# Decoder layer on one core: low key parts of the score products padded with zero rows to 128, one buffer for attended rows, scorer row reloaded per batch

## What is computed

```python
h = x * rsqrt(mean(x * x, -1) + EPS) * norm_w        # x is layer-normed before
q, k, v = proj(w_q), proj(w_k), proj(w_v)            # 16 heads of 64
ll = where(causal, einsum('qd,kd->qk', q, k) * 64 ** -0.5, NEG)
scores = h @ scorer_w + scorer_b
idx = top_k(scores, 128)                             # these keys count a second time
attn = softmax(concat([ll, ll at idx]))
o = attn[:512] @ v + attn[512:] @ v[idx]
x = x + x + o @ w_out                                # layer-normed x inside
```

## Time and profile before

| | us |
|---|---|
| three runs: median (lowest, highest) | 2413.64 (2413.43, 2414.61) |
| profiled execution: span from first to last instruction | 2414.0 |
| PE busy in the span | 2241.6 (93%) |
| DVE busy | 1349.6 (56%) |
| ACT busy | 845.5 (35%) |
| POOL busy | 429.2 (18%) |

### The profile page before, as it was taken

How to read it: one execution, slowest core, us unless ns; L and a number is a source line. 1 busy time by engine, 2 the same in 40 slices (tenths; PEclk the granted TensorE clock), 3 DMA queues, 4 the chain that set the end, 5 groups by cost and what they waited for, 6 DMA issues and landing times. The chain is left out here.

```text
span 2414.0 us, 35686 instructions
## 1 busy us (share of the span) xinstructions
PE 2241.6 (93%) x12029; PEld 1682.4 (70%) x12029; DVE 1349.6 (56%) x3145; ACT 845.5 (35%) x1541; POOL 429.2 (18%) x669
## 2 busy tenths in 40 slices
PE   3999999999999999999999999996898888878899
PEld 3786777678678677767767767773787888865543
DVE  4574376177257437617725743661787878845500
ACT  3442344144144234314414423441644444413210
POOL 2100000010010000001001000002866666620000
PEclk9999999999999999999999999997988888858999
DMA  5000000100100000010010000002013211141000
GB/s 183 1 1 31 23 1 10 45 1 1 54 1 1 31 23 1 10 45 1 1 54 1 1 28 27 1 10 91 29 56 102 83 55 55 53 152 50 1 0 18
DMA packets 46136, 80.23 MB, mean 33 GB/s; under 512 B 10067, under 2 KB 10067, under 8 KB 45448
## 3 DMA queue, kind: packets, MB, share of 16 engines
q1 hardware_dynamic: 45320, 75.85, 9.3%
q0 software_dynamic: 640, 2.10, 0.2%
HBM read 60.11 MB, written 17.83 MB: 32 GB/s over the span
## 5 line engine op out<-in xcount | busy, mean ns | idle before, releaser
L405 ACT ACTIVATE probs<-s_bank,nmax 128x512 f32<-128x512 f32 (+3 forms) x512 | 249.4, 525 | 421.6 <-DVE nmax L530 294.3
L530 DVE TENSOR_REDUCE nmax<-s_bank 128x1 f32<-128x512 f32 (+2 forms) x384 | 185.3, 510 | 305.7 <-PE s_bank L665 302.0
L688 PE MATMUL o_bank<-vals,probs_t 128*128 128x65 f32 x2560 | 322.2, 269 | 0.0
L688 PEld LDWEIGHTS o_bank<-vals,probs_t 128*128 128x128 f32 x2560 | 311.0, 192 | 1.4 <-DVE probs_t L538 1.4
L712 PE MATMUL pj_bank<-w_o,o_t 128*128 128x512 f32 x512 | 223.5, 597 | 6.0 <-ACT o_t L413 6.0
L538 DVE COPY probs_t<-pt_bank 128x512 f32<-128x512 f32 x320 | 218.0, 681 | 3.6 <-PE pt_bank L673 3.6
L319 POOL TENSOR_TENSOR idle<-ones 128x4 f32<-128x4 f32 x41 | 8.1, 198 | 1065.7 <-DMA probs<-in_x 1063.7
L673 PE MATMUL pt_bank<-ident,probs 128*128 128x128 f32 x1280 | 194.1, 274 | 0.0
L712 PEld LDWEIGHTS pj_bank<-w_o,o_t 128*128 128x128 f32 x512 | 97.2, 191 | 127.6 <-issue 127.6
L664 PE MATMUL s_bank<-k_lo,q_both 64*128 64x512 f32 (+3 forms) x448 | 184.9, 413 | 0.0
L514 DVE SCALAR_TENSOR_TENSOR q_both<-pj_bank,q_both 64x512 fp32r<-64x512 f32 x128 | 88.2, 689 | 141.6 <-ACT q_both L392 138.9
(11 more groups left out here) (266 smaller groups left out, 4245.5 us busy)
## 6 DMA issues: line engine op xcount, KB each, us to landing
xb<-in_x SPq DMA_DIRECT2D x9, 1024.0 KB, 5.3
xt<-x SPq DMA_DIRECT2D x36, 256.0 KB, 2.8
probs<-in_x SPq DMA_DIRECT2D x32, 256.0 KB, 2.7
x<-probs SPq DMA_DIRECT2D x32, 256.0 KB, 2.0
am<-in_L_ffn_attention_mask SPq DMA_DIRECT2D x8, 1024.0 KB, 5.2
out<-x SPq DMA_DIRECT2D x32, 256.0 KB, 2.1
w_sb<-in_L_ffn_w SPq DMA_DIRECT2D x2, 4096.0 KB, 20.2
o_t<-in_L_attn_w_v SPq DMA_DIRECT2D x2, 1024.0 KB, 9.5
```

Source lines behind the costliest of these rows:

```text
L405: ins = nc.scalar.activation(probs[:, i % 2, c0:c0 + nk], s_bank[i % 2][:, c0:c0 + nk], ACT.Exp, bias=nmax[:, i % 4, n:n + 1])
L530: ins = nc.vector.tensor_reduce(nmax[:, i % 4, n:n + 1], s_bank[i % 2][:, c0:c0 + nk], AX.X, ALU.max, negate=True)
L688: ins = nc.tensor.matmul(o_bank[slot][:, o0:o0 + VW], probs_t[:, i % 2, c0 + P * kt:c0 + P * kt + P], vals[:, kt, 2 * p + h, :], start=(kt ...
```

## The change

The low key part moves to a tile `k_second` of 2 x 2 x 512 columns on 128 rows: for each head its own 64 rows hold the low part and the other 64 hold zeros, which a single memset writes at the start. The low product uses all 128 rows, with the same query tile as the high product, and the order high, low, causal is the same in all units; `s_half` is gone. `o_norm` has one buffer instead of two, and the scorer row shares the tile of `row_s`: it is kept in DRAM (`sw_kept`) and loaded anew to all partitions in each batch, once the rank counts that read `row_s` are through. With one `o_norm`, "ot" stands one round earlier, between "t" and "pv" of unit 3's round (g = 8, 13, ...), and in a batch's last rounds ahead of the last "ht". DVE waits for "ot" before it divides the next pair's first unit.

```diff
--- before.py
+++ after.py
@@ -98,6 +98,8 @@
             plan.append(("s", g))
         if 2 <= g < NU + 2:
             plan.append(("t", g - 2))
+        if g >= 8 and (g - 8) % UNITS == 0:
+            plan.append(("ot", (g - 8) // UNITS))
         if 3 <= g < NU + 3:
             plan.append(("pv", g - 3))
         if g < NU and p + 1 < NPAIR and u < 4:
@@ -112,9 +114,6 @@
             plan.append(("rank", RANK_AT.index(g)))
         if NU <= g < NU + DC:
             plan.append(("ht", g - NU))
-        if g >= 9 and (g - 9) % UNITS == 0 and (g - 9) // UNITS < NPAIR - 1:
-            plan.append(("ot", (g - 9) // UNITS))
-    plan.append(("ot", NPAIR - 1))
     plan += [("out", t) for t in range(TT)]
     return plan
 
@@ -147,22 +146,24 @@
 
 
         q_both, k_twice = sb("q_both", [P, 2, 2, S], F32R), sb("k_twice", [P, 2, 2, S], F32R)
-        k_lo = sb("k_lo", [P, 2, S], F32R)
+        k_second = sb("k_second", [P, 2, 2, S], F32R)
         probs = sb("probs", [P, 2, 512])
         probs_t = sb("probs_t", [P, 2, 512])
         o_rden = sb("o_rden", [P, 2, 2])
-        o_norm = sb("o_norm", [P, 2, TT, 2, HD])
+        o_norm = sb("o_norm", [P, TT, 2, HD])
         o_t = sb("o_t", [P, NPAIR, S])
         xr = probs
+        norm_row = probs[:, 0, :]
         ident = sb("ident", [P, P])
         ident_b = sb("ident_b", [P, P], BF16)
         causal_b = sb("causal_b", [P, P], BF16)
         before = sb("before", [P, S + P * (TT - 1)], I8)
         row_s = sb("row_s", [P, S])
+        sw = row_s
+        sw_kept = nc.dram_tensor("sw_kept", [1, D], F32, kind="Internal").ap()
         junk = sb("junk", [P, S], BF16)
         carrier = sb("carrier", [P, 4])
         nw = sb("nw", [P, DC])
-        sw = sb("sw", [P, D])
         sbias = sb("sbias", [P, 1])
         bn = sb("bn", [P, TT, 6])
         mv = sb("mv", [P, TT, 2])
...
@@ -250,15 +251,25 @@
             with nc.allow_non_contiguous_dma(reason="one column per chunk"):
                 sp.dma_start(nw[:, :], norm_w.rearrange("(c p) -> p c", p=P)).then_inc(small_in, 16)
             sp.dma_start(sw[:, :], scorer_w.rearrange("d o -> o d").broadcast_to((P, D))).then_inc(small_in, 16)
-            sp.dma_start(row_s[:, :], norm_w.rearrange("(o d) -> o d", o=1).broadcast_to((P, D))).then_inc(small_in, 16)
+            sp.dma_start(norm_row, norm_w.rearrange("(o d) -> o d", o=1).broadcast_to((P, D))).then_inc(small_in, 16)
             sp.dma_start(sbias[:, :], scorer_b.rearrange("(o d) -> o d", o=1).broadcast_to((P, 1))
                          ).then_inc(small_in, 16)
             for i, (n, hw) in enumerate(W_ORDER):
+                if i == 2:
+                    sp.wait_ge(sw_made, 1)
+                    sp.dma_start(sw_kept[:, :], sw[0:1, :]).then_inc(sw_out, 16)
                 if i >= 2:
                     sp.wait_ge(split_lo, i - 1)
                 sp.dma_start(o_t[:, DC * (i % 2):DC * (i % 2) + DC, :],
                              w_dram[n][:, :, 512 * hw:512 * hw + 512]).then_inc(w_loaded[i % 2], 16)
             sp.dma_start(w_o[:, :, :], w_out.rearrange("(c p) d -> p c d", p=P)).then_inc(wo_in, 16)
+
+            def scorer_again(b):
+
+                sp.wait_ge(twice_ready, b + 1)
+                sp.dma_start(sw[:, :], sw_kept.broadcast_to((P, D))).then_inc(sw_in, 16)
+
+            sp.wait_ge(sw_out, 16)
 
             def results(b):
 
...
@@ -430,9 +443,11 @@
                     ins = nc.vector.bn_aggr(mv[:, t, :], bn[:, t, :])
                 ins.then_inc(stats_ready, 1)
 
-            def dot(n):
+            def dot(b, n):
 
                 dv.wait_ge(h_ready, n * TT + TT)
+                if b is not None:
+                    dv.wait_ge(sw_in, b * 16 + 16)
                 for t in range(TT):
                     step(nc.vector.tensor_tensor_reduce(junk[:, :], xb[:, t, :], sw[:, :], 1.0, 0.0, ALU.mult,
                                                              ALU.add, score[:, t:t + 1]))
...
@@ -477,19 +494,20 @@
                 nc.vector.tensor_tensor(w_lo[n][:, :, cols], o_t[:, DC * (i % 2):DC * (i % 2) + DC, :],
                                         w_hi[n][:, :, cols].bitcast(F32), ALU.subtract).then_inc(split_lo, 1)
 
+            nc.vector.memset(k_second[:, :, :, :].bitcast(F32), 0.0).then_inc(const_made, 1)
             dv.wait_ge(const_made, N_CONST)
 
             for i, at_one in enumerate((y_ready, *x1_out)):
                 nc.vector.memset(carrier[:, 1 + i:2 + i], 0.0).then_inc(at_one, 1)
             stats(0)
             dv.wait_ge(small_in, 64)
-            nc.vector.tensor_tensor(sw[:, :], sw[:, :], row_s[:, :], ALU.mult).then_inc(sw_made, 1)
+            nc.vector.tensor_tensor(sw[:, :], sw[:, :], norm_row, ALU.mult).then_inc(sw_made, 1)
             dv.wait_ge(sw_made, 1)
             split(0)
             split(1)
             for c in range(DC):
                 normed(None, 0, c)
-            dot(0)
+            dot(None, 0)
             split(2)
             score_row(None, 0)
             split(3)
@@ -515,7 +533,7 @@
                                                                      HD ** -0.5, q_both[own, i % 2, h, :].bitcast(F32),
                                                                      ALU.mult, ALU.subtract)
                             else:
-                                ins = nc.vector.tensor_tensor(k_lo[own, i % 2, :], pj_bank[slot][own, :],
+                                ins = nc.vector.tensor_tensor(k_second[own, i % 2, h, :], pj_bank[slot][own, :],
                                                               k_twice[own, i % 2, h, :].bitcast(F32), ALU.subtract)
                         ins.then_inc(qk_lo, 1)
                     if kind == "s":
@@ -539,16 +557,16 @@
                     if kind == "pv":
                         p, u = divmod(i, UNITS)
                         dv.wait_ge(pv_ready, b * NU + i + 1)
-                        if u == 0 and p >= 2:
-                            dv.wait_ge(pt_ready, pt(b, ("ot", p - 2))[1])
+                        if u == 0 and p >= 1:
+                            dv.wait_ge(pt_ready, pt(b, ("ot", p - 1))[1])
                         n = len(unit_blocks(u))
                         src = o_bank[i % 2][:, 0:n * VW].rearrange("p (n v) -> p n v", n=n)
                         if u < 2:
-                            dst = o_norm[:, p % 2, 3:4, u, :]
+                            dst = o_norm[:, 3:4, u, :]
                         elif u < 4:
-                            dst = o_norm[:, p % 2, 0:3:2, u - 2, :]
+                            dst = o_norm[:, 0:3:2, u - 2, :]
                         else:
-                            dst = o_norm[:, p % 2, 1, :, :]
+                            dst = o_norm[:, 1, :, :]
                         step(nc.vector.reciprocal(o_rden[:, i % 2, 0:n], src[:, :, HD]))
                         nc.vector.tensor_tensor(dst, src[:, :, 0:HD],
                                                 o_rden[:, i % 2, 0:n].unsqueeze(2).broadcast_to((P, n, HD)),
...
@@ -650,18 +668,11 @@
                         if i >= 2:
                             pe.wait_ge(p_ready, b * NU + i - 1)
                         for h, t, c0, nk in unit_blocks(u):
-                            queries, rows = slice(P * t, P * t + P), head_rows(h)
-                            high = (q_both[:, p % 2, h, queries], k_twice[:, p % 2, h, 0:nk])
-                            low = (q_both[rows, p % 2, h, queries], k_lo[rows, p % 2, 0:nk])
-                            if u == UNITS - 1 and h == 0:
-                                nc.tensor.matmul(s_bank[slot][:, c0:c0 + nk], *low, start=True, stop=False
-                                                 ).then_inc(s_half, 1)
-                                nc.tensor.matmul(s_bank[slot][:, c0:c0 + nk], *high, start=False, stop=False)
-                            else:
-                                nc.tensor.matmul(s_bank[slot][:, c0:c0 + nk], *high, start=True, stop=False)
-                                if u == UNITS - 1:
-                                    pe.wait_ge(s_half, b * NPAIR + p + 1)
-                                nc.tensor.matmul(s_bank[slot][:, c0:c0 + nk], *low, start=False, stop=False)
+                            queries = q_both[:, p % 2, h, P * t:P * t + P]
+                            nc.tensor.matmul(s_bank[slot][:, c0:c0 + nk], queries, k_twice[:, p % 2, h, 0:nk],
+                                             start=True, stop=False)
+                            nc.tensor.matmul(s_bank[slot][:, c0:c0 + nk], queries, k_second[:, p % 2, h, 0:nk],
+                                             start=False, stop=False)
                             ins = nc.tensor.matmul(s_bank[slot][:, c0 + nk - P:c0 + nk], ident_b[:, :], causal_b[:, :],
                                                    start=False, stop=True)
                         ins.then_inc(s_ready, 1)
...
```

(14 more changed lines are left out.)

## The result

The kernel after takes 2290.87 us (median of four runs, 2288.05 to 2291.84) against 2414.12 us for the kernel before on the same chip: a ratio of 0.9476 [0.9455, 0.9497]. That is 123 us less, where 135 were forecast.

The account below looks back on a forecast made before the run. The prediction took PE's instructions as the bound. Scores -149, waits +13, the batch's DVE work +7 and batch ends -6 gave -135 us, from 2414.0 to 2279 us, range 2254 to 2325, chance 0.74.

Parts of the forecast that it names:

- Score products: Score units: low products on 128 instead of 64 rows gain 2.32 us per pair, 149 us in 64 pairs.
- What is late next: Rounds without a projection: PE waits for DVE's low key part and copy, 0.2 us per pair, 13 us.
- The walk: From unit 3's scores on, engine by engine: low key part ends at 4.27 us, the copy at 5.5.
- The batch's own DVE work: Rounds 14 and 18: DVE's dot and score copy delay PE, 0.9 us per batch, 7 us.
- The moved transposes and the batch's end: o_norm transposes never wait in rounds; the 0.8 us wait before each output projection goes, 6 us gained.
- Edits at nothing: Removed s_half wait, k_second memset at the start and scorer reload per batch cost nothing; uncovered memset 2.8 us once.
- (a): Units 3 and 4: DVE and ACT become the bound, PE waits about 1 us per pair; 2330 us, chance 0.11.
- (b): Full-row product behind one with the same stationary tile exposes its load, 51 us in all; 2330 us, chance 0.06.
- (c): Score steps do not come from the row count, and 128 padded rows keep them; 2401 us, chance 0.06.
- (d): PE stands at the o_norm transposes until DVE divides a pair's last unit; slower, 2434 us, chance 0.03.

Follow-up runs that it names:

- 64-row variant: The kernel after with only its low products put back on the 64 rows of their head, and the wait in unit 4 with them: 2400.93 us.

## Why the prediction was right, point by point

**Score products.** Right in mechanism and nearly in size: 2.21 us per pair against 2.32, some 7 us in all. The low products take 0.23, 0.18, 0.12 and 0.11 us as read from the 64-row steps. The sum failed in "0.18 and 0.125 for 384 and 256" for the three high products of a pair that stand behind a short causal one: 0.26 (657.85 to 658.11) and 0.20. They last 0.42 and 0.36 us where the low ones last 0.33 and 0.28. The weight load of the first is recorded from 657.82 to 658.02, so it ends 0.17 us after its product's start (657.85); the low one's, from 657.94, ends 0.02 after its own (658.11). So I take it that a part of their load stays in view; this was not tried by itself. The high product of 128 columns, 0.06 instead of 0.11, gives a part back.

**What is late next.** This is the term that was mis-sized. The walk had the chain right, with the two waits where they came, but it handed work from engine to engine too early. From unit 3's start (657.64) it put the division at 2.5, the low key part's end at 4.27 and the copy's at 5.5. They came at 2.72, 4.45 and 5.76. PE itself is 0.09 later than in the walk: its scores take 0.71 us for 0.68, and the `o_norm` transposes 0.44 for 0.37. The division starts 0.32 us after PE has gone on to unit 4 (660.04), where the walk had about 0.2: the attended products' recorded end (660.23) is 0.19 behind that start, and DVE follows another 0.13 later. Unit 0 too follows the low key part by 0.12 us (662.09 to 662.21), where the walk had hardly 0.1, and the copy was counted as 0.6 us where the earlier trace rows have 0.68. So the waits are 0.15 and 0.17, and a restart of 0.09 behind the second that I did not have, 0.41 instead of 0.2 us per pair. The `o_norm` transposes cost 0.07 more than where they stood. Together 0.48 us in the 56 pairs that prepare keys for another, 27 us where 13 were forecast.

**The batch's own DVE work.** Near in size by luck: about 0.6 us per batch against 0.9. The dot costs 0.15 us. The pair of rounds 20 to 24 loses 0.25, which the sum did not have: DVE stands for 0.29 us between the two instructions of one division (710.05 to 710.34), at the same place in every batch, for a reason that the trace does not show. The round with the score loses 0.5 us ahead of its "t", not through DVE's copy but through the bank ring: the score's transposes push "t" to the bank of "ot", and ACT copies that only at 693.61 to 694.20, behind its key copies. In return that pair's usual waits are some 0.3 us shorter. PE's and ACT's timelines there:

```profile
693.78 0.23 PE L676 MATMUL s_bank<-causal_b,ident_b 128*128 128x128 bf16 x1
694.35 0.63 PE L684 MATMUL pt_bank<-ident,probs 128*128 128x128 f32 x4 [0.33 <-ACT o_t L426]
```
```profile
693.61 0.59 ACT L426 COPY o_t<-pt_bank 128x512 f32<-128x512 f32 x1
```

**The moved transposes and the batch's end.** Right: no wait at `o_norm` inside the rounds, and 0.97 us per batch at the end, 7.8 us against 6. In the rounds the order's cost is the 0.07 above.

**Edits at nothing.** The reload is shown to be hidden. The memset took 1.76 us, from 1.31 us on, and DVE's next instruction starts at 4.40 instead of 4.39 us, so it is covered. The lost `s_half` was not tried alone. The first scores start at 75.77 us instead of 74.5, but at 74.07 and 76.15 in the two other profiled executions of the same kernel, so this does not tell a cost from scatter.

**The sum.** 64 x 2.21 = 141 us, less 56 x 0.48 = 27 and 8 x 0.6 = 5, and 8 x 0.97 = 8 and the one longer batch end of before, 1.7, on top, less 1.3 for the later first scores: 118 of the 119.7 us up to the last output projection. The forecast of 135 us had the scores at 149, the waits at 13, the batch's work at 7 and its end at 6.

**The rivals.** (a), DVE and ACT as the bound, is half true: the wait exists at 0.4 us per pair, not at 1, because the q projection lets DVE catch up each time. (b), exposed loads behind the same stationary tile, falls: the low products stand there, and none of them shows it. What may be exposed is the load of the three high products of 384 and 256 columns behind causal ones, some 0.08 us each. (c) falls with the low steps of 0.23 us and with the 64-row variant at 2400.93, (d) with the `o_norm` transposes that never wait in a round.

## What to carry to other kernels

Before a product is put on fewer rows, count how often TensorE changes its row count: here each trip there and back cost 0.28 us, and padding with zero rows to the full 128 was cheaper than half the rows. When the bound engine gets shorter, walk the next engine's chain from the recorded end of what releases it, not from the start of the next instruction, and add the handover: here 0.13 us from PE's end to DVE's start and 0.12 back. A wait that hangs on an engine without slack only moves if one order is changed: with the `o_norm` transposes back in their old place it stood one step on, and with the low key part done earlier the wait for it went, but the one for the copy behind it stayed.

## What the hardware showed that I had not expected

With two 64-row products in a row a batch is shorter than with one between 128-row ones (198.3 against 200.2 us), and the second lasts 0.39 us where the first lasts 0.49. A float32 product of 384 or 256 columns behind a 128-column bfloat16 one took 0.26 and 0.20 us, the one with the same columns behind it 0.18 and 0.12. And two idle times of PE of 0.84 and 0.75 us at a batch's end were followed, in three of seven batches, by an output projection at a granted clock of 0.79 over its first 8 us, 1.7 us lost at a time; with the order of the kernel after there was none in 88 batch ends.
